# VectorE's state update moved ahead of its wait for GpSimd's power in the LSTM step

## The chip, the cores and the metric

One core of one Trainium2 chip runs the whole kernel, once. The metric is device microseconds for that launch; lower is better. Times given as a median are over 3 runs, and the profile is one further execution with its own time.

## What is computed

A vision-transformer-like tower over 128 images of 3 x 224 x 224: patches are projected to tokens, an LSTM runs over the 65 tokens of each image, and a mixture of 16 experts (top 2) follows. Cut to what matters:

```python
tokens = einsum('bpi,hi->bph', patches, W) + b           # 64 patches of 3*28*28 = 2352 values, 128 outputs
h0 = concat([cls, tokens], axis=1) * pos_embed            # 65 tokens
xg = einsum('btd,gd->btg', layernorm(h0), W_ih) + b_ih + b_hh
def step(carry, xt):                                      # 65 steps, one after the other
    h, c = carry
    i, f, g, o = split(xt + h @ W_hh.T, 4)
    c = sigmoid(f) * c + sigmoid(i) * tanh(g)
    h = sigmoid(o) * tanh(c)
    return (h, c), h
h1 = h0 + lstm                                            # residual
out = h1 + experts(layernorm(h1))                         # router, top 2 of 16, gelu in between
```

## The kernel before

The batch of 128 images fills the partitions. Each engine has a program of its own, written out by hand, and the engines meet only through semaphores; `through(engine, s, t)` waits until semaphore `s` has reached t + 1. Every engine runs its instructions strictly in the order of its program, so a wait holds up all that stands behind it.

The first 65 steps (n = 0 to 64) are the LSTM stage. A step n of the program works on several tokens at once, which is a software pipeline: token n in the LSTM recurrence, token n+1 and n+2 in the normalisation and the input gates, token n+3 in the patch projection, token n-1 and n-2 in the residual, the second normalisation and the router. From n = 61 the expert tiles join in, 80 tiles of 256 rows, and after the last step they run alone.

What each engine does in step n, in the order of its program:

- **TensorE**: the recurrent matmuls of token n (L1073 reads `h2_hi`, L1078 reads `h2_lo`), the transposition of the state h(n-1) (L1088), the transposition of the normalised row of token n-2 (L1098), the input-gate matmuls of token n+1 (L1106), the patch projection of token n+3 (L1063, 46 or more matmuls, the bulk of the step), the transposition of the normalised input `xn` of token n+2 (L1142), and the router (L1154). Just ahead of L1098 stands the wait for `xT_lo_done` of token n+1, so TensorE stops there when VectorE's `xT_lo` isn't ready.
- **ScalarE**: four tanh for the gates (L501), a copy `ynT` (L510), the first half of the split of the patches into two float16 parts (L484), the tanh of the cell `tc` (L520), the second half of the split (L484), the normalised row `pay` of token n-1 (L531, which needs `shift2`), the copy `xT_hi` (L538), and two copies of a piece of the expert weights (L544 and L545), which wait for that piece's DMA `ex_raw`. The gates of the next step stand behind them.
- **VectorE**: `xT_lo` (L639), the router's logits (now and then), the input row (L655), the residual row (L661), the statistics of both (L665 to L674), variance plus epsilon `veps` (L679), then `cab` and the cell `c2` (L683 and L686), then a wait for GpSimd's `rstd_done`, `shift2` (L690) and `xn` (L695), then the state as `h2_hi` (float16), `h2` and `h2_lo` (L700, L702, L706) behind a wait for `tc_done`, then `xlo` (L713), and last pieces of the routing (L762 and after, in most steps some three to five instructions). The next step begins with `xT_lo` again.
- **GpSimd**: `ex_lo` of a piece of the weights (L1001), the power -0.5 that gives `rstd` for two rows at once (L1008, waits for `veps`), and up to four indirect DMAs that send rows to the experts' lists (L1030).
- **SyncE** issues the loads: the patches of token n+6 (L365, L368, 1.2 MB), the positions (L391), the piece of weights n (L400).

The order of the state update against the normalised input is the order of the VectorE program in `step(n)`; nothing else decides it.

Of the kernel before, what the change touches and what calls it, by code (L numbers as in the profile page):

```python
# [83 lines left out]
def tower(nc, x, w, w_rest, cls, pos, w_ih, w_hh, b_ih, b_hh, rw, rb, we, b1, b2, const, out):  # L84
    F32, F16, I32 = mybir.dt.float32, mybir.dt.float16, mybir.dt.int32
    ALU, ACT, AX = mybir.AluOpType, mybir.ActivationFunctionType, mybir.AxisListType
    ctx = ExitStack()
    with ctx:
        def sb(name, shape, dt=F32):
            return ctx.enter_context(nc.sbuf_tensor(name, shape, dt))  # L90

        def sem(name):
            return ctx.enter_context(nc.semaphore(name))
# [34 lines left out]
        mv = sb("mv", [P, 2, 2])  # L128
        veps = sb("veps", [P, 2])
        rstd = sb("rstd", [P, 2])  # L130
        shift2 = sb("shift2", [P, 2])
        xn = sb("xn", [P, 2, HID])
# [113 lines left out]
        h0_done, xn_done = sem("h0_done"), sem("xn_done")  # L246
        st1, st2, moments = sem("st1"), sem("st2"), sem("moments")
        veps_done, rstd_done, shift_done = sem("veps_done"), sem("rstd_done"), sem("shift_done")
        xT_ps, xT_hi_done, xT_lo_done = sem("xT_ps"), sem("xT_hi_done"), sem("xT_lo_done")
# [86 lines left out]
        def through(eng, s, t):  # L336
            eng.wait_ge(s, (t + 1))

        def norms(n):

            there = [k for k, t in ((0, n + 2), (1, n - 1)) if 0 <= t <= T - 1]
            return slice(there[0], there[-1] + 1) if there else None

        def normed(n):

            return (n + 3)
# [250 lines left out]
        def _(dve):  # L597
# [37 lines left out]
            def step(n):  # L635
# [8 lines left out]
                t0, t1 = n + 2, n - 1  # L644
                pre, post = 0 <= t0 <= T - 1, 0 <= t1 <= T - 1
                if pre:

                    src0 = h0[:, t0 % 4, :]
# [26 lines left out]
                both = norms(n)  # L675
# [4 lines left out]
                if 0 <= n <= T - 1:  # L680
# [3 lines left out]
                                             ALU.mult).then_inc(cab_done, 1)  # L684
                    through(dve, cab_done, n)
                    dve.scalar_tensor_tensor(c2, cab[:, 0, :], 0.5, cab[:, 1, :], ALU.mult, ALU.add).then_inc(c_done, 1)  # L686
                if both:
                    dve.wait_ge(rstd_done, normed(n))
                if post:
                    dve.scalar_tensor_tensor(shift2[:, t1 % 2:t1 % 2 + 1], mv[:, 1, 0:1], -1.0, rstd[:, 1:2], ALU.mult,  # L690
                                             ALU.mult).then_inc(shift_done, 1)
                if pre:
                    if t0 >= 2:
                        through(dve, xT_ps, t0 - 2)
                    dve.tensor_scalar(xn[:, t0 % 2, :], src0, mv[:, 0, 0:1], rstd[:, 0:1], ALU.subtract,  # L695
                                      ALU.mult).then_inc(xn_done, 1)
                if 0 <= n <= T - 1:

                    through(dve, tc_done, n)
                    dve.scalar_tensor_tensor(h2_hi[:, n % 2, :], gate[:, 2, :], 1.0, tc[:, :], ALU.add,  # L700
                                             ALU.mult).then_inc(h_hi_done, 1)
                    dve.scalar_tensor_tensor(h2[:, n % 2, :], gate[:, 2, :], 1.0, tc[:, :], ALU.add,  # L702
                                             ALU.mult).then_inc(h_done, 1)
                    through(dve, h_hi_done, n)
                    through(dve, h_done, n)
                    dve.tensor_tensor(h2_lo[:, n % 2, :], h2[:, n % 2, :], h2_hi[:, n % 2, :],  # L706
                                      ALU.subtract).then_inc(h_lo_done, 1)
                t = n + 4
                if 1 <= t <= T - 1:

# [248 lines left out]
            def below_most():  # L959
# [3 lines left out]
                dve.tensor_tensor(top[:, 1, :], top[:, 1, :], top[:, 0, :], ALU.subtract).then_inc(under, 1)  # L963

            slots(step, step_b)

            dve.wait_ge(exp_done, 1)
# [304 lines left out]
```

## Time and profile before

| | |
|---|---|
| runs | 732.04 us median of 3 (730.67 to 735.34) |
| profiled execution | 732.84 us; its span from the first to the last instruction is 731.0 us |
| mean granted TensorE clock | 0.959 |
| TensorE, matmul | 630.0 us busy, 86% of the span |
| TensorE, weight load | 591.4 us, 81% |
| VectorE | 575.6 us, 79% |
| ScalarE | 488.3 us, 67% |
| GpSimd | 412.5 us, 56% |
| chain of work that ended last | TensorE 69%, issue 9%, DMA 7%, VectorE 5%, GpSimd 4% |

The LSTM stage takes the first 430 us or so of the span, the expert tiles most of the rest, and a last stage gathers the experts' results. The busy shares are averages over these stages. In the chain, "issue" is time for which the profile shows no releaser.

### The profile page before, as it was taken

How to read it: one execution, taken by the hardware profiler on the slowest of the kernel's cores; microseconds unless marked ns; L12 is line 12 of the kernel's file. 1: busy time of each engine (PE TensorE's matmuls, PEld its weight loads, DVE VectorE, ACT ScalarE, POOL GpSimd, SP SyncE). 2: the span in 40 equal slices, each digit the busy share in tenths (PEclk: the TensorE clock that was granted, in tenths of full speed). 3: DMA queues.
4: the chain of work that ended last, by engine and by line, in shares of the span. 5: the costliest groups of instructions: out<-in, count | busy, mean ns of one | idle time of the engine just before them, and what ended most of it. 6: DMA issues, size and time to landing. Idle time of an engine off the chain costs nothing.

```text
span 731.0 us, 25050 instructions
## 1 busy us (share of the span) xinstructions
PE 630.0 (86%) x7952; PEld 591.4 (81%) x7952; DVE 575.6 (79%) x1839; ACT 488.3 (67%) x1335; POOL 412.5 (56%) x446
## 2 busy tenths in 40 slices
PE   3999999999999999898988758899899999999500
PEld 3989989999989999898988737787799899899400
DVE  4577888787987887888888858887788888888587
ACT  4366666666666666666565556787788888888565
POOL 0122224766766767668367767777666666676600
PEclk9999999999999999999999969999999999999955
DMA  8767777877777778778674322455443333343097
GB/s 320 277 233 250 239 237 233 261 247 260 254 253 250 250 248 263 237 235 262 210 250 141 82 57 76 123 153 147 139 116 113 105 109 105 99 116 94 13 375 322
DMA packets 72188, 141.72 MB, mean 194 GB/s; under 512 B 13110, under 2 KB 55682, under 8 KB 63870
## 3 DMA queue, kind: packets, MB, share of 16 engines
q1 hardware_dynamic: 62416, 121.69, 52.2%
q0 software_dynamic: 9280, 17.21, 6.6%
q8 instruction: 70, 1.15, 0.6%
q10 hardware_dynamic: 366, 1.21, 0.5%
q14 instruction: 56, 0.46, 0.2%
HBM read 116.35 MB, written 25.66 MB: 194 GB/s over the span
## 4 chain that ended last, share of the span: by engine, by line
PE 69%; issue 9%; DMA 7%; DVE 5%; POOL 4%; SPq 2%; ACT 2%; POOLq 0%; ACTq 0%; DVEq 0%
PE bank L1063 28%; PE bank L1206 13%; PE bank L1223 12%; PE bank L1106 5%; PE bank L1073 3%; POOL sent L1030 3%; DMA patches<-back 2%; PE bank L1180 2%; DMA ex_raw<-in_we 2%; PE bank L1078 2%; PE bank L1098 2%; DMA patches<-in_x 1%; DMA patches<-sent 1%; PE bank L1154 1%; PE bank L1142 1%
## 5 line engine op out<-in xcount | busy, mean ns | idle before, releaser
L1041 POOL DMA_INDIRECT back<-patches x160 | 156.7, 979 | 70.7 <-issue 57.5
L1063 PE MATMUL bank<-ws,patches 128*128 128x128 f32 (+1 forms) x1408 | 176.7, 283 | 11.5 <-DMA patches<-in_x 11.5
L1030 POOL DMA_INDIRECT sent<-pay,slot_own x130 | 156.6, 1205 | 40.4 <-issue 39.8
L1063 PEld LDWEIGHTS bank<-ws,patches 128*128 128x128 f32 (+1 forms) x1408 | 167.4, 197 | 11.8 <-issue 9.2
L556 ACT ACTIVATE bank<-bank,b1s 128x256 f32<-128x256 f32 x320 | 130.9, 453 | 46.5 <-PE bank L1206 46.4
L918 DVE TENSOR_TENSOR patches<-bank,patches 128x512 f16<-128x512 f32 x160 | 109.7, 686 | 30.4 <-ACT patches L565 22.7
L1206 PE MATMUL bank<-patches,ex_hi 128*128 128x256 f16 x640 | 113.0, 278 | 5.0 <-POOL ex_lo L1001 2.9
L1223 PE MATMUL bank<-ex_hi,patches 128*128 x1280 | 111.7, 219 | 3.7 <-DVE patches L934 3.1
L1001 POOL TENSOR_TENSOR ex_lo<-ex_raw,ex_hi 128x256 f16<-128x256 f32 x64 | 44.2, 690 | 111.7 <-ACT ex_raw L545 111.5
L565 ACT ACTIVATE patches<-bank 128x512 f16<-128x512 f32 x160 | 97.6, 611 | 0.0
L1223 PEld LDWEIGHTS bank<-ex_hi,patches 128*128 128x128 f16 x1280 | 87.1, 98 | 8.0 <-issue 5.4
L1063 PE MATMUL bank<-whi,xhi 128*128 128x128 f16 x512 | 89.6, 220 | 0.0
L1063 PE MATMUL bank<-whi,xlo 128*128 128x128 f16 x512 | 89.3, 219 | 0.0
L1063 PE MATMUL bank<-wlo,xhi 128*128 128x128 f16 x512 | 89.3, 219 | 0.0
L1206 PE MATMUL bank<-patches,ex_lo 128*128 128x256 f16 x320 | 88.7, 277 | 0.0
L1223 PE MATMUL bank<-ex_lo,patches 128*128 x640 | 88.0, 219 | 0.0
L1008 POOL TENSOR_TENSOR rstd<-veps,cst 128x2 f32<-128x2 f32 (+1 forms) x68 | 52.6, 773 | 56.2 <-DVE veps L679 55.2
L484 ACT ACTIVATE xhi<-patches 128x512 f16<-128x512 f32 x128 | 80.5, 631 | 1.9 <-DMA patches<-in_x 1.7
L538 ACT ACTIVATE xT_hi<-bank 128x128 f16<-128x128 f32 x65 | 18.0, 276 | 90.9 <-PE bank L1142 87.2
L713 DVE TENSOR_TENSOR xlo<-patches,xhi 128x1024 f16<-128x1024 f32 x64 | 78.5, 1226 | 0.2
L1206 PEld LDWEIGHTS bank<-patches,ex_hi 128*128 x640 | 56.3, 99 | 24.2 <-issue 14.5
L501 ACT ACTIVATE gate<-bank,lbias 128x128 f32<-128x128 f32 x260 | 73.5, 364 | 2.3 <-PE bank L1078 2.3
(139 smaller groups left out, 1439.0 us busy)
## 6 DMA issues: line engine op xcount, KB each, us to landing
patches<-in_x SPq DMA_DIRECT2D x64, 1152.0 KB
patches<-sent SPq DMA_DIRECT2D x80, 130.0 KB
patches<-back SPq DMA_DIRECT2D x13, 640.0 KB, 6.4
ex_raw<-in_we SPq DMA_DIRECT2D x64, 128.0 KB
patches<-in_b SPq DMA_DIRECT2D x80, 64.0 KB
posr<-in_pos SPq DMA_DIRECT2D x65, 64.0 KB
out_tower<-h SPq DMA_DIRECT2D x13, 320.0 KB, 5.1
back<-patches POOLq DMA_INDIRECT x160
```

The lines of the kernel that those rows point to most:

```text
L484: return act.activation(xhi[r][:, a:b, :], xraw[q][:, a:b, :], ACT.Copy)
L501: last = act.activation(gate[:, GATE_AT[g], :], ps_gate[n % 2][:, g * B:(g + 1) * B], ACT.Tanh, bias=lbias[:, 2, g:g + 1], scale=(1.0 if g ...
L556: last = act.activation(up[:, cols], up[:, cols], ACT.Gelu, bias=b1s[:, bass.ds(e * FC + 2 * half + i, 1)], scale=1.0 / E_SCALE)
L565: act.activation(hhi[n % 4][:, half * 512:(half + 1) * 512], ps_up(n, half)[:, :], ACT.Copy).then_inc(hhi_done, 1)
L713: dve.tensor_tensor(xlo[r][:, :, :], xraw[q][:, 0:KS, :], xhi[r][:, :, :], ALU.subtract).then_inc(lo_done, 1)
L918: dve.tensor_tensor(hlo[n % 4][:, cols], ps_up(n, half)[:, :], hhi[n % 4][:, cols], ALU.subtract).then_inc(hlo_done, 1)
L1008: pool.tensor_tensor(rstd[:, both], veps[:, both], cst[:, C_POW:C_POW + 1].to_broadcast([P, both.stop - both.start]), ALU.pow).then_inc(rs ...
L1030: pool.indirect_dma_start(sent, bass.IndirectOffsetOnAxis(ap=slot_own[:, g % 4, k, col:col + 1], axis=0), pay[:, t % NP, :], None, bounds_ ...
L1041: pool.indirect_dma_start(back, bass.IndirectOffsetOnAxis(ap=dsti[j % NO][:, k:k + 1], axis=0), yo[j % NO][:, k, :], None, bounds_check=2 ...
L1063: last = pe.matmul(bank_of, l, w_, start=(c == KS and k == 0), stop=(c == KS - 1 and k == 2))
L1206: last = pe.matmul(ps_up(n, half)[:, i * ROWS:(i + 1) * ROWS], w1, r, start=(k == 0), stop=(k == 2))
L1223: last = pe.matmul(ps_down(j)[:, a * HID:(a + 1) * HID], h, w2, start=(c == 0 and k == 0 and a == 0), stop=(c == FC - 1 and k == 2), skip_ ...
```

## The change

In VectorE's `step(n)` the block that writes the state (`h2_hi`, `h2`, `h2_lo`) is moved from behind `shift2` and `xn` to a place ahead of the wait for `rstd_done`. The same instructions run with the same operands and the same waits; none is added or taken away, and the programs of the other engines stay as they were.

```diff
@@ -684,6 +684,17 @@
                     dve.scalar_tensor_tensor(c2, cab[:, 0, :], 0.5, cab[:, 1, :], ALU.mult, ALU.add).then_inc(c_done, 1)
+                if 0 <= n <= T - 1:
+
+                    through(dve, tc_done, n)
+                    dve.scalar_tensor_tensor(h2_hi[:, n % 2, :], gate[:, 2, :], 1.0, tc[:, :], ALU.add,
+                                             ALU.mult).then_inc(h_hi_done, 1)
+                    dve.scalar_tensor_tensor(h2[:, n % 2, :], gate[:, 2, :], 1.0, tc[:, :], ALU.add,
+                                             ALU.mult).then_inc(h_done, 1)
+                    through(dve, h_hi_done, n)
+                    through(dve, h_done, n)
+                    dve.tensor_tensor(h2_lo[:, n % 2, :], h2[:, n % 2, :], h2_hi[:, n % 2, :],
+                                      ALU.subtract).then_inc(h_lo_done, 1)
                 if both:
                     dve.wait_ge(rstd_done, normed(n))
                 if post:
@@ -694,17 +705,6 @@
                         through(dve, xT_ps, t0 - 2)
                     dve.tensor_scalar(xn[:, t0 % 2, :], src0, mv[:, 0, 0:1], rstd[:, 0:1], ALU.subtract,
                                       ALU.mult).then_inc(xn_done, 1)
-                if 0 <= n <= T - 1:
-
-                    through(dve, tc_done, n)
-                    dve.scalar_tensor_tensor(h2_hi[:, n % 2, :], gate[:, 2, :], 1.0, tc[:, :], ALU.add,
-                                             ALU.mult).then_inc(h_hi_done, 1)
-                    dve.scalar_tensor_tensor(h2[:, n % 2, :], gate[:, 2, :], 1.0, tc[:, :], ALU.add,
-                                             ALU.mult).then_inc(h_done, 1)
-                    through(dve, h_hi_done, n)
-                    through(dve, h_done, n)
-                    dve.tensor_tensor(h2_lo[:, n % 2, :], h2[:, n % 2, :], h2_hi[:, n % 2, :],
-                                      ALU.subtract).then_inc(h_lo_done, 1)
```

## Rows read from the trace of the kernel before

**Rows 1.** Busy time, 100 to 200 us (PE, PEld, DVE, ACT, POOL, clock, DMA share, GB/s)

```profile
100.00:200.00 100.00, 95.11 (x1238) 93.32 (x1237) 82.51 (x296) 64.70 (x200) 60.62 (x65) 1.00 0.75 249
```

**Rows 2.** TensorE's waits, whole span (us in total, times, longest)

```profile
PE bank L1098 <- issue: 24.4, 24, 2.3
PE bank L1073 <- DVE h_hi L700: 2.7, 1, 2.7
```

**Rows 3.** VectorE's and ScalarE's waits, from 30 to 400 us

```profile
DVE cab L683 <- ACT gate L501: 28.0, 24, 2.3
DVE shift L690 <- POOL rstd L1008: 11.6, 33, 1.9
...
ACT ex_hi L544 <- DMA ex_raw<-in_we: 35.5, 35, 2.6
```

**Rows 4.** Timeline, VectorE and TensorE, step 43 (start us, us, engine, line)

```profile
290.98 0.43 DVE L683 SCALAR_TENSOR_TENSOR cab<-gate 128x256 f32<-128x256 f32 x1 [1.60 <-ACT gate L501]
...
291.44 0.29 DVE L686 SCALAR_TENSOR_TENSOR gate<-cab 128x128 f32<-128x128 f32 x1
...
292.11 0.29 DVE L700 SCALAR_TENSOR_TENSOR h_hi<-gate,tc 128x128 f16<-128x128 f32 x1
...
292.81 0.28 PE L1142 MATMUL bank<-cst,xn 128*128 128x128 f32 x1
...
292.92 1.28 DVE L713 TENSOR_TENSOR xlo<-patches,xhi 128x1024 f16<-128x1024 f32 x1
...
295.48 0.28 DVE L639 TENSOR_TENSOR xT_lo<-bank,xT_hi 128x128 f16<-128x128 f32 x1
...
295.86 0.30 PE L1098 MATMUL bank<-cst,pay 128*128 128x128 f32 x1 [1.84 <-issue]
```

**Rows 5.** First and last of the 17 stalls behind an early step, TensorE's timeline

```profile
39.65 0.30 PE L1098 MATMUL bank<-cst,pay 128*128 128x128 f32 x1 [0.91 <-DVE xT_lo L639]
...
379.86 0.30 PE L1098 MATMUL bank<-cst,pay 128*128 128x128 f32 x1 [1.57 <-issue]
```

**Rows 6.** Timeline, GpSimd and VectorE, step 49 and (last row) step 50

```profile
328.62 0.85 POOL L1001 TENSOR_TENSOR ex_lo<-ex_raw,ex_hi 128x256 f16<-128x256 f32 x1
...
328.98 0.64 DVE L686 SCALAR_TENSOR_TENSOR gate<-cab 128x128 f32<-128x128 f32 x1
...
330.23 0.16 DVE L690 SCALAR_TENSOR_TENSOR shift<-mv,rstd 128x1 f32<-128x1 f32 x1 [0.62 <-POOL rstd L1008]
...
330.57 0.28 DVE L700 SCALAR_TENSOR_TENSOR h_hi<-gate,tc 128x128 f16<-128x128 f32 x1
...
331.37 1.22 DVE L713 TENSOR_TENSOR xlo<-patches,xhi 128x1024 f16<-128x1024 f32 x1
...
335.21 0.16 DVE L690 SCALAR_TENSOR_TENSOR shift<-mv,rstd 128x1 f32<-128x1 f32 x1 [0.29 <-POOL rstd L1008]
```

**Rows 7.** Timeline, step 51, and TensorE's stall at the head of step 52

```profile
340.31 0.29 DVE L686 SCALAR_TENSOR_TENSOR gate<-cab 128x128 f32<-128x128 f32 x1
...
341.77 0.72 POOL L1008 TENSOR_TENSOR rstd<-veps,cst 128x2 f32<-128x2 f32 x1
...
342.53 0.16 DVE L690 SCALAR_TENSOR_TENSOR shift<-mv,rstd 128x1 f32<-128x1 f32 x1 [1.92 <-POOL rstd L1008]
...
343.66 1.22 DVE L713 TENSOR_TENSOR xlo<-patches,xhi 128x1024 f16<-128x1024 f32 x1
...
346.88 0.45 PE L1098 MATMUL bank<-cst,pay 128*128 128x128 f32 x1 [2.30 <-issue]
```

**Rows 8.** Busy time in the stretch behind that stall (clock 0.63)

```profile
346.90:351.00 4.10, 4.10 (x30) 4.05 (x31) 3.64 (x15) 2.13 (x5) 2.43 (x3) 0.63 0.72 261
```

**Rows 9.** Timeline around steps 63 and 64: VectorE, GpSimd, TensorE

```profile
422.61 0.16 DVE L690 SCALAR_TENSOR_TENSOR shift<-mv,rstd 128x1 f32<-128x1 f32 x1 [2.24 <-POOL rstd L1008]
...
428.26 0.70 POOL L1001 TENSOR_TENSOR ex_lo<-ex_raw,ex_hi 128x256 f16<-128x256 f32 x1
...
429.96 0.60 PE L1206 MATMUL bank<-patches,ex_hi 128*128 128x256 f16 x2 [2.95 <-POOL ex_lo L1001]
```

## The prediction

> **What bounds the kernel now.** I read the busy shares and the chain first: TensorE leads, with 69% of the chain. I then read the stages. In the LSTM stage TensorE is 95% busy and VectorE 83%, at the full clock, 2.4 GHz [rows 1]. So a step lasts what TensorE's own work needs, plus its stalls. TensorE's waits say where these are: 24 times, 24.4 us in total, ahead of L1098 [rows 2]. The profile names no releaser for them, but the program does: ahead of L1098 stands the wait for `xT_lo`, the first instruction of VectorE's step. Laid side by side, VectorE writes `xT_lo` from 295.48 to 295.76 us and TensorE goes on at 295.86 after 1.84 us of idle time [rows 4]. TensorE isn't waiting for the state; it waits for VectorE to reach the end of its step.
>
> VectorE's waits tell why it is late [rows 3]. In 24 steps between 30 and 400 us `cab` waited for the gates, because ScalarE had waited for a piece of the expert weights (35 waits, 35.5 us). I call these steps **early**, since in them `rstd` is there before `c2`. In 33 steps VectorE waited for `rstd`: 11.6 us in all. The timelines split these into 30 waits of at most 0.30 us, as in step 50, and three **late** ones: 0.62 us in step 49, 1.92 in step 51 and 0.62 in step 57, when GpSimd's row sends and `ex_lo` ran over [rows 6, 7]. Step 61 repeats step 49.
>
> **The change, part by part.** Nothing is added; only VectorE's order changes. I measure how long VectorE needs from the end of `c2` to the start of `xlo`.
>
> - Before, early step: 292.92 - 291.73 = 1.19 us [rows 4]. `tc` takes ScalarE's tanh, so `h2_hi` can't start before 0.38 us after `c2` (292.11 - 291.73), and `shift2` and `xn` fill just this gap. The three state instructions then take 0.81 us.
> - `shift2` and `xn` cost VectorE 330.57 - 330.23 = 0.34 us [rows 6].
> - After: 0.38 us of idle time, 0.81 for the state, 0.34 for `shift2` and `xn`: 1.53 us, unless `rstd` comes later than 1.19 us after `c2`.
>
> So an early step gets 0.34 us longer: the filler is taken out of the gap. An ordinary step (0.29 us of wait, then 331.37 - 330.23 = 1.14 us from `shift2` to `xlo`, together 1.43) gets 0.10 longer [rows 6]. Step 49 took 331.37 - 329.62 = 1.75 us and gets 0.22 shorter, and 57 and 61 likewise. Step 51 took 343.66 - 340.60 = 3.06 us; with `shift2` at 342.53 and 0.34 behind it, it takes 2.27, so 0.79 shorter [rows 7].
>
> What reaches TensorE depends on the slack ahead of `xT_lo`. I went through the timelines of all steps. 17 of the 24 early steps are followed by a stall, so that VectorE's end sets it (the first and the last in [rows 5]): 17 x 0.34 = 5.8 us. The other seven have 0 to 0.5 us of slack; I take 1.2 us for them together. Most ordinary steps have 0.1 to 1.6 us of slack before ScalarE's `xT_hi` is there; some seven have none: 0.5 us. The late steps give back 3 x 0.22 + 0.79 = 1.5 us.
>
> The stall of 2.30 us at the head of step 52 is followed by a stretch with a granted clock of 0.63 [rows 7, 8], that is, partly at 1.2 GHz. TensorE is busy for all of its 4.10 us, so the clock costs 4.10 x (1 - 0.63) = 1.5 us. With 0.79 us less, its stall is 1.5 us, and behind the stalls of 1.84 us [rows 4] and 1.57 [rows 5] the clock stayed full. I count this 1.5 us as won.
>
> Queued behind the moved instructions: `xn` now ends some 1.6 us after `c2`, and TensorE reads it at L1142. In ordinary steps that is over a microsecond early enough. In ten early steps it is late, as in step 43: 291.73 + 1.6 = 293.35 against 292.81 [rows 4]. TensorE then stalls 0.1 to 1.25 us in front of L1142. That costs nothing more, since TensorE stalls anyway a little later for `xT_lo`, and that stall shrinks by the same amount; in all ten it is long enough or short by under 0.1. ScalarE's `pay` waits for `shift2`, now about 0.9 us later, and `xT_hi` and the copies of the weights stand behind it; in ordinary steps ScalarE has 1.5 us idle there. GpSimd's program doesn't wait for what moved. SyncE's patch load waits for `xlo` of two steps before, and its queue is unaffected.
>
> At the end of the stage VectorE waited 2.24 us for `rstd` in step 63, and TensorE 2.7 us for `h2_hi` [rows 2, 9]. That wait goes, but the expert tiles start when GpSimd has written the last `ex_lo`, 428.96 us, behind its row sends; TensorE then resumes at 429.96 [rows 9]. What is late next is GpSimd, so 2.7 us of stall are worth nothing. In step 64 VectorE does 0.8 us of state work ahead of time, of which TensorE sees 0.15 to 0.2.
>
> Sum: 5.8 + 1.2 + 0.5 - 1.5 - 1.5 - 0.2 = **+4.3 us**. The profiled execution took 732.84 us and would take 737.1. It lies 0.8 above the median of 732.04, so for a median I forecast **736.3 us**.
>
> One rule speaks against the gain of the late steps. The trace first: L686 took 0.64 us in step 49, where GpSimd's `ex_lo` was running, and 0.29 in step 51 [rows 6, 7]. The Trainium skill, SBUF — State Buffer, "Who interferes with whom", says that a VectorE instruction with two SBUF inputs contends with a GpSimd instruction that reads SBUF, and that the later one waits. The trace agrees. By that rule the state instructions, moved beside the power, would lengthen by up to 0.35 us in steps 49, 57 and 61, and the sum would be +5.3 instead of +4.3.
>
> **The rivals.**
>
> - *The DMA sets the pace.* If the weight pieces land at their own rate, each 0.34 us added to a step shortens a later wait of ScalarE. The 35 waits [rows 3] could absorb all 7.5 us, and the gains of 3.2 stay: 732.04 - 3.2 = 728.8 us, on the faster side. It decides once more than 4.3 of the 7.5 is absorbed. For it: DMA is 75% busy [rows 1], and the waits come every two or three steps. Against it: a load is issued relative to TensorE's step, and most waits are longer than 0.34 us and recur after stalls that cleared the queues.
> - *More stalls cross into the lower clock.* Steps 12, 43 and 56 would stall 2.0, 2.2 and 1.8 us, between 1.84 (full clock) and 2.30 (0.63). Each crossing costs 1.5 us; with two, and no gain at step 52: 736.3 + 4.5 = 740.8 us.
> - *The wait for `xn` adds up.* If it doesn't come out of the later stall, ten waits of 0.6 us on average cost 6 us or more: 742 us or above. Against it: `xT_lo` hangs on VectorE's end, not on L1142, in these steps.
> - *GpSimd is late far more often than this execution shows.* Each step like 51 gives 0.8 us and perhaps 1.5 of clock; it takes five more of them to be over 1% faster. The trace has one.
>
> **How the numbers follow.** My forecast, 733 to 739 us: 0.50. Absorbed by the DMA, 728.8 to 733: 0.25. Clock or added waits, above 739: 0.20. Late GpSimd, below 728.8: 0.05. The range takes in most of the first three, 729.5 to 741.5. About 1%, 7.3 us, is what a measurement of this kernel can tell from no change. Below 724.7: 0.05. Above 739.4: 0.16. Within: 0.79.
>
> **What would show it.** In the profile after, each early step should have 1.53 us from `c2` to `xlo`, with 0.38 idle ahead of `h2_hi`. VectorE's wait for `rstd` at L690 should all but vanish, being left in steps 51, 63 and 64. TensorE should have new waits ahead of L1142, and those at L1098 should not shrink by more than that. The clock behind step 51 should stay full. I am wrong if the weights' waits fall by some 4 us or more, if the clock dips elsewhere, or if TensorE's total stall in the LSTM stage doesn't grow by about 6 us.

## The result, and the profile after

| | before | after |
|---|---|---|
| median | 733.87 us (728.96 to 738.33, 15 runs) | 738.01 us (733.85 to 743.10, 15 runs) |
| ratio of the two | | 1.005, 95% interval 1.0028 to 1.0073 |
| profiled execution | 732.84 us, span 731.0 | 735.97 us, span 734.2 |
| mean granted TensorE clock | 0.959 | 0.956 |

The change makes the kernel 4.1 us slower (738.01 - 733.87); 4.3 us were forecast. It is inside the 1% that the prediction called no change, but the interval leaves 1.000 out. The ratios here and below leave out the few executions that were slow as a whole, so they need not equal the quotient of two medians.

In the kernel after, `h2_hi`, `h2` and `h2_lo` are L690, L692 and L696, `shift2` is L701 and `xn` L706. First one early step, to hold against [rows 4]. The timeline of the kernel after, VectorE and TensorE, step 43 (start us, us, engine, line, operation, in brackets the idle time before it and what ended it):

```profile
294.22 0.42 DVE L683 SCALAR_TENSOR_TENSOR cab<-gate 128x256 f32<-128x256 f32 x1 [1.24 <-ACT gate L501]
294.68 0.29 DVE L686 SCALAR_TENSOR_TENSOR gate<-cab 128x128 f32<-128x128 f32 x1
295.34 0.29 DVE L690 SCALAR_TENSOR_TENSOR h_hi<-gate,tc 128x128 f16<-128x128 f32 x1 [0.38 <-ACT tc L520]
296.15 0.15 DVE L701 SCALAR_TENSOR_TENSOR shift<-mv,rstd 128x1 f32<-128x1 f32 x1
296.22 0.34 DVE L706 TENSOR_SCALAR xn<-h,mv,rstd 128x128 f32<-128x128 f32 x1
...
296.48 1.22 DVE L713 TENSOR_TENSOR xlo<-patches,xhi 128x1024 f16<-128x1024 f32 x1
...
296.61 0.33 PE L1142 MATMUL bank<-cst,xn 128*128 128x128 f32 x1
...
298.81 0.28 DVE L639 TENSOR_TENSOR xT_lo<-bank,xT_hi 128x128 f16<-128x128 f32 x1
...
299.19 0.30 PE L1098 MATMUL bank<-cst,pay 128*128 128x128 f32 x1 [1.32 <-issue]
```

VectorE stands 0.38 us idle ahead of `h2_hi` for the tanh behind `c2`, and `h2_hi` begins at the same distance as before. From the end of `c2` (294.97) to `xlo` (296.48) it is 1.51 us, where it was 1.19. The gap that `shift2` and `xn` filled is now empty, and they are paid for behind it. TensorE still stops ahead of L1098 until VectorE's `xT_lo` is there.

VectorE's, TensorE's and ScalarE's waits in the kernel after, from 30 to 400 us (us in total, times, longest), to hold against [rows 3] and, for L1098, [rows 2]:

```profile
ACT ex_hi L544 <- DMA ex_raw<-in_we: 30.1, 31, 2.3
ACT pay L531 <- DVE shift L701: 29.0, 57, 0.5
...
DVE cab L683 <- ACT gate L501: 26.8, 26, 2.4
...
DVE h_hi L690 <- ACT tc L520: 22.1, 59, 0.4
PE bank L1098 <- issue: 16.0, 15, 2.8
...
PE bank L1142 <- DVE xn L706: 4.7, 8, 1.3
```

VectorE's wait for `rstd`, 11.6 us in 33 steps before, is gone from this stretch altogether. What took its place is larger: 22.1 us in 59 steps, the tanh's gap, which was full of work before. ScalarE's `pay` now waits for `shift2`. TensorE has a new wait ahead of L1142, as forecast, and the one ahead of L1098 is smaller by about as much. The steps that VectorE's lateness starts in are still there (26 waits of `cab` for the gates).

Where the 4 us lie can be read off the start of the first recurrent matmul (L1073) of a step. The last column is ScalarE's waits for the weights up to step 47. "e1" to "e12" are the experiments below:

| kernel | step 1 to 48 | 48 to 54 | 54 to 64 | start of 64 | waits for weights |
|---|---|---|---|---|---|
| before | 287.7 | 39.2 | 64.1 | 423.0 | 29.7 us, 28 |
| after | 292.3 | 36.6 | 66.0 | 426.0 | 24.4, 22 |
| e1, before, weights early | 271.0 | 37.7 | 64.3 | 405.4 | none |
| e2, after, weights early | 272.2 | 35.4 | 63.0 | 401.8 | none |
| e3, before, power twice | 294.6 | 41.8 | 71.8 | 441.1 | 25.0, 25 |
| e4, after, power twice | 292.5 | 40.0 | 64.1 | 428.2 | 29.6, 29 |
| e5, third order, weights early | 271.0 | 36.8 | 63.8 | 403.6 | none |
| e6, third order | 298.2 | 37.7 | 66.0 | 433.0 | 33.2, 26 |
| e7, before, power first, weights early | 282.2 | 37.5 | 66.0 | 416.8 | none |
| e8, third order, power first, weights early | 290.5 | 41.8 | 69.8 | 432.9 | none |
| e9, after again | 302.9 | 42.0 | 66.3 | 442.4 | 28.0, 24 |
| e10, before again | 292.5 | 38.1 | 66.9 | 428.5 | 31.7, 24 |
| e11, before, 0.34 us more on VectorE | 300.1 | 42.2 | 67.8 | 442.2 | 31.6, 28 |
| e12, third order again | 295.9 | 37.9 | 66.0 | 432.3 | 30.8, 29 |

In the first pair the change costs 4.6 us up to step 48, where the early and ordinary steps are, gains 2.6 between 48 and 54, where GpSimd was late before, and loses 1.9 behind that: together 3.9 us. The start of step 64 moves by 3.0 us only and the span by 3.2, because step 1 started 1.0 us sooner in this execution (31.1 against 32.1 us). Step 0 already did (25.3 against 26.3), ahead of the first use of the moved block, so that 1.0 us is not of the change.

The loss from 54 to 64 has a place of its own. TensorE's timeline in the kernel after, at the head of step 57, and its busy time ahead of that stall and behind it (PE, PEld, DVE, ACT, POOL, granted clock, DMA share, GB/s):

```profile
382.70 0.30 PE L1098 MATMUL bank<-cst,pay 128*128 128x128 f32 x1 [2.83 <-issue]
```

```profile
372.00:381.90 9.90, 7.87 (x111) 7.62 (x108) 8.37 (x29) 6.07 (x19) 7.17 (x9) 1.00 0.76 218
381.90:386.00 4.10, 3.30 (x22) 3.33 (x23) 3.52 (x17) 1.79 (x5) 2.25 (x3) 0.62 0.72 278
```

This is the dip of [rows 8] (0.63), moved from step 52 to step 57: TensorE stood idle for 2.83 us and its clock then averaged 0.62, so part of that stretch ran at 1.2 GHz. Over step 57 it averaged 0.83, which over the step's 10.3 us is a loss of 1.7 us. Behind step 51 the clock stayed at its full 2.4 GHz, as forecast. Part of that long stall is a piece of the routing that met GpSimd. VectorE's and GpSimd's timelines of the kernel after:

```profile
380.90 1.37 DVE L870 TENSOR_TENSOR tabs<-tabs 128x16 f32<-128x16 f32 x2
...
381.55 0.69 POOL L1001 TENSOR_TENSOR ex_lo<-ex_raw,ex_hi 128x256 f16<-128x256 f32 x1
```

The same two instructions took 0.38 us in step 55. Beside `ex_lo` they took 1.37 us, and `xT_lo` stands behind them.

### The profile page after: what moved, and what is told of

It reads as the page before. It is cut to its first block, busy times and chain, and to the rows that moved or that the text cites. A ratio compares the mean times of both kernels' runs of the same rounds, so it can differ in the third digit from the quotient of the medians.

```text
span 734.2 us, 25050 instructions
## 1 busy us (share of the span) xinstructions
PE 632.9 (86%) x7952; PEld 592.1 (81%) x7952; DVE 576.2 (78%) x1839; ACT 494.0 (67%) x1335; POOL 406.6 (55%) x446
## 4 chain that ended last, share of the span: by engine, by line
PE 28%; DMA 6%; issue 5%; DVE 4%; SPq 3%; POOL 2%; ACT 2%; POOLq 0%; ACTq 0%; DVEq 0%
PE bank L1206 13%; PE bank L1223 12%; DMA patches<-back 3%; PE bank L1180 2%; POOL sent L1030 2%; DMA patches<-sent 1%; DMA ex_raw<-in_we 1%; ACT patches L592 1%; SPq L428 0%; DVE h L986 0%; SPq L437 0%; SPq L409 0%; SPq L410 0%; SPq L438 0%; SPq L429 0%
## 5 line engine op out<-in xcount | busy, mean ns | idle before, releaser
L1063 PE MATMUL bank<-ws,patches 128*128 128x128 f32 (+1 forms) x1408 | 176.2, 282 | 11.6 <-DMA patches<-in_x 11.6
L1030 POOL DMA_INDIRECT sent<-pay,slot_own x130 | 150.0, 1154 | 40.5 <-issue 38.6
L918 DVE TENSOR_TENSOR patches<-bank,patches 128x512 f16<-128x512 f32 x160 | 109.6, 685 | 30.8 <-ACT patches L565 23.8
```

The source lines that it names most:

```text
L918: dve.tensor_tensor(hlo[n % 4][:, cols], ps_up(n, half)[:, :], hhi[n % 4][:, cols], ALU.subtract).then_inc(hlo_done, 1)
L1030: pool.indirect_dma_start(sent, bass.IndirectOffsetOnAxis(ap=slot_own[:, g % 4, k, col:col + 1], axis=0), pay[:, t % NP, :], None, bounds_ ...
L1063: last = pe.matmul(bank_of, l, w_, start=(c == KS and k == 0), stop=(c == KS - 1 and k == 2))
```

## Experiments

Each ratio is to the kernel before, run on the same chip in the same series. On the chips of e5 to e8 and e9 to e12 the kernel before itself took 837.37 and 840.10 us (medians), against 733.87 and 737.15 on the first two; nearly all of the difference lies behind the LSTM stage (last section). So times of different series are not compared, only ratios and the stages of the table above.

### Are the early steps the cause? e1 and e2: weights loaded one step sooner

Early steps exist because ScalarE waits for a piece of the expert weights. Both kernels get the same edit in SyncE's program; e1 has VectorE's order of before, e2 that of the change:

```diff
-                if 0 <= n <= PIECES - 1:
-                    if n >= 4:
-                        through(sp, ex_lo_done, n - 4)
-                    sp.dma_start(ex_raw[:, n % 4, :], we[:, bass.ds(n * PIECE, PIECE)]
-                                 ).then_inc(ex_in[n % 4], 16)
+                piece = n + 1
+                if 0 <= piece <= PIECES - 1:
+                    if piece >= 4:
+                        through(sp, ex_lo_done, piece - 4)
+                    sp.dma_start(ex_raw[:, piece % 4, :], we[:, bass.ds(piece * PIECE, PIECE)]
+                                 ).then_inc(ex_in[piece % 4], 16)
```

> The kernel before, but SyncE issues the load of each piece of the expert weights one step earlier. My theory: ScalarE's waits for these pieces (35.5 us in 35 waits) make the early steps, in which the gates come late while rstd is ready. They should all but vanish (under 5 us), the 24 waits of cab for the gates too, and the time should fall by 8 to 18 us. Rival, the DMA sets the pace: the waits move elsewhere and the time falls by less than 3 us.

> The same earlier load, with the changed order. My theory: the change costs 0.34 us in early steps and 0.08 to 0.10 in ordinary ones with mostly slack behind them. Without early steps it should cost no more than 2 us against the kernel before with the earlier load, and could gain 1. Rival: the cost is there in every step, whether or not the gates are late; then the 4 us stay.

Measured: e1 715.70 us (714.73 to 718.48, 4 runs), ratio 0.9722 (0.9644 to 0.9801). e2 713.25 us (710.96 to 713.70, 4 runs), ratio 0.9680 (0.9606 to 0.9754). Both beat both kernels. e1's time fell by 21.5 us (737.15 - 715.70), more than the 8 to 18 expected. The ranges of the runs of e1 and e2 do not overlap, though they are of four runs each, and the changed order is now the faster one by 2.4 us, where 1 at most had been expected.

Waits from 30 to 400 us, first e1, then e2 (all lines lie 1 higher than in before and after):

```profile
DVE shift L691 <- POOL rstd L1009: 21.3, 62, 1.9
...
PE bank L1099 <- issue: 8.5, 7, 2.4
```

```profile
DVE h_hi L691 <- ACT tc L521: 23.3, 62, 0.4
...
PE bank L1099 <- issue: 5.9, 6, 2.0
```

Neither kernel has a wait of ScalarE for weights or of `cab` for gates: every step is ordinary or late. Up to step 48 the changed order still costs 1.2 us (272.2 against 271.0). From 48 to 54 it gains 2.3 and from 54 to 64 1.3. So without early steps the sign turns, as the prediction's sum has it: its 7.0 us from early steps fall out, and the 0.5 of the ordinary and the gains of the late ones stay.

### Does the change do what it says where GpSimd is late? e3 and e4: the power computed twice

GpSimd computes the power once more into a spare tile ahead of the real one. This is extra work; nothing is left out. e3 has the order of before, e4 that of the change:

```diff
+                    pool.tensor_tensor(spare[:, both], veps[:, both],
+                                       cst[:, C_POW:C_POW + 1].to_broadcast([P, both.stop - both.start]),
+                                       ALU.pow)
```

> The kernel before, with GpSimd computing the power once more into a spare tile ahead of the real one, so that rstd comes 0.7 to 0.8 us later in every step. My theory: ordinary steps wait some 1.0 us at L690 instead of 0.3 and the time grows by 8 to 20 us. Rival: VectorE's wait doesn't reach TensorE and the time grows by under 3 us.

> The same doubled power, with the changed order. My theory: rstd now comes about 1.0 us after c2, still ahead of the 1.19 us at which the state is written, so nothing more is waited for; the time is 737 to 741 us, 6 to 15 us below the doubled power in the old order. That is where the change pays. Rival: the change costs its 4 us whatever rstd does, and the time is 4 us above that of the old order with the doubled power.

Measured: e3 754.40 us (749.70 to 757.92, 4 runs), ratio 1.0238 (1.0139 to 1.0336). e4 740.03 us (735.76 to 744.15, 10 runs), ratio 1.0042 (1.0006 to 1.0078). The changed order is 14.4 us faster here.

The waits of e3 from 30 to 400 us, and one of them in VectorE's timeline; then the same wait in e4:

```profile
DVE shift L691 <- POOL rstd L1012: 45.2, 57, 2.6
```

```profile
242.91 0.16 DVE L691 SCALAR_TENSOR_TENSOR shift<-mv,rstd 128x1 f32<-128x1 f32 x1 [0.96 <-POOL rstd L1012]
```

```profile
DVE shift L702 <- POOL rstd L1012: 1.8, 2, 0.9
```

With `rstd` 0.96 us after `c2` instead of 0.29, the order of before pays 45.2 us of waiting, and the changed order 1.8: its state work covers up to 1.19 us. The rival that the change costs its 4 us whatever `rstd` does falls. But the waits on VectorE are not what reaches the end: between step 1 and 48, where most of the 45.2 us lie, the two profiled executions are only 2.1 us apart (294.6 and 292.5), while 1.8 us lie between 48 and 54 and 7.7 between 54 and 64, where GpSimd is late. Up to step 48 the rest falls into time in which TensorE didn't need VectorE, or comes off ScalarE's waits for the weights, which are 4.6 us shorter in e3 than in e4; the runs don't part the two. What the change lacks in the real kernel is a wait to cover: 0.29 us, less than the 0.38 us that the tanh takes anyway.

### Is it the order, or the late `xn`? e6, e5 and e12: a third order

The state's first two instructions go ahead of the wait for `rstd`, and `h2_lo` stays behind `xn`. So `shift2` and `xn` stand between `h2` and `h2_lo`, which waits for `h2` in any case:

```diff
+                if 0 <= n <= T - 1:
+
+                    through(dve, tc_done, n)
+                    dve.scalar_tensor_tensor(h2_hi[:, n % 2, :], gate[:, 2, :], 1.0, tc[:, :], ALU.add,
+                                             ALU.mult).then_inc(h_hi_done, 1)
+                    dve.scalar_tensor_tensor(h2[:, n % 2, :], gate[:, 2, :], 1.0, tc[:, :], ALU.add,
+                                             ALU.mult).then_inc(h_done, 1)
                 if both:
                     dve.wait_ge(rstd_done, normed(n))
...
                 if 0 <= n <= T - 1:
-
-                    through(dve, tc_done, n)
-                    dve.scalar_tensor_tensor(h2_hi[:, n % 2, :], gate[:, 2, :], 1.0, tc[:, :], ALU.add,
-                                             ALU.mult).then_inc(h_hi_done, 1)
-                    dve.scalar_tensor_tensor(h2[:, n % 2, :], gate[:, 2, :], 1.0, tc[:, :], ALU.add,
-                                             ALU.mult).then_inc(h_done, 1)
                     through(dve, h_hi_done, n)
```

e6 is this alone, e5 has the weights a step early too.

> Weights one step early, and a third order: h2_hi and h2 ahead of the wait for rstd as in the changed kernel, then shift2 and xn, and h2_lo behind them, so that shift2 and xn fill the 0.18 us in which h2_lo waits for h2. My theory: from c2 to xlo it takes 1.35 us, against 1.51 in the changed order and 1.43 in ordinary steps of the old one; with VectorE's end setting about a third of the steps this gives 1 to 4 us over the changed order with the early weights (713.2). Rival: TensorE has slack there, and the time is the same within 1 us.

> The third order alone, with the weights loaded as before. My theory: early steps cost 1.35 us against 1.19 before and 1.51 in the changed kernel, ordinary and late ones are shorter than before: the time lies 0 to 2 us above the kernel before, at least 1 us below the changed one. Rival, the loss of the change isn't the VectorE time of the early steps but the late xn or the late state: then it is as slow as the changed kernel, or slower since the state's low part comes later still.

Measured: e5 810.64 us (809.26 to 813.65, 4 runs), ratio 0.9664 (0.9630 to 0.9699). e6 840.63 us (834.59 to 843.78, 10 runs), ratio 1.0030 (1.0000 to 1.0059). From `c2` to `xlo` both take 1.31 us, 0.20 less than the changed order: the time in which `h2_lo` waited for `h2` is now used. e6 lies 0.30% above the kernel before, some 2.5 us, a little over the 0 to 2 expected, and its interval overlaps that of the change (1.0028 to 1.0073): by itself it doesn't tell the third order from the changed one. e5 has the lowest ratio of all, but its interval covers e2's 0.9680, so which of the two is better is not settled.

e12 repeats e6 beside the kernel after (e9), the kernel before (e10) and e11, all on one chip.

> The third order with the weights loaded as before, on the chip of the changed kernel's repeat. My theory: 1 to 3 us below the changed kernel, since from c2 to xlo it takes 1.31 us against 1.51. Rival, the late state and xn themselves cost: not below it.

Measured: 838.82 us (835.50 to 845.90, 10 runs), ratio 0.9986 (0.9959 to 1.0013), against 1.0096 for e9: the third order is as fast as the kernel before within 0.4%, and about 1.1% faster than the changed order on the same chip, with intervals that do not meet. 1 to 3 us had been expected; 1.1% is 9 us. So the third order doesn't win: it undoes the loss. `xn` ends 154.04 - 152.84 = 1.20 us after `c2` in it, where the changed order has 296.56 - 294.97 = 1.59 (step 43 above); before, TensorE could already use it 292.81 - 291.73 = 1.08 us after `c2` [rows 4]. VectorE's timeline of e12, an early step:

```profile
152.55 0.29 DVE L687 SCALAR_TENSOR_TENSOR gate<-cab 128x128 f32<-128x128 f32 x1
153.22 0.29 DVE L691 SCALAR_TENSOR_TENSOR h_hi<-gate,tc 128x128 f16<-128x128 f32 x1 [0.38 <-ACT tc L521]
...
153.63 0.15 DVE L698 SCALAR_TENSOR_TENSOR shift<-mv,rstd 128x1 f32<-128x1 f32 x1
153.70 0.34 DVE L703 TENSOR_SCALAR xn<-h,mv,rstd 128x128 f32<-128x128 f32 x1
```

### How much of added VectorE time arrives? e9, e10 and e11

e9 is the kernel after again, e10 the kernel before again (one run). e11 is the kernel before with one more VectorE instruction, shaped like `xn` and written to a spare tile, behind `h2_lo` in every step:

```diff
+                    if n >= 1:
+                        dve.tensor_scalar(spare[:, :], h1[:, n - 1, :], mv[:, 0, 0:1], rstd[:, 0:1], ALU.subtract,
+                                          ALU.mult)
```

> The changed kernel once more, so that it stands on one chip with the three others here. Theory: a ratio of 1.003 to 1.007 to the kernel before.

> The kernel before once more, for its profile on this chip, to see how far the count of early steps and stalls (24 and 17 in the first profile, ScalarE's waits for the weights 35.5 us) repeats. Theory: 20 to 30 early steps, waits of 30 to 42 us, first recurrent matmul of step 48 within 4 us of 320 us.

> The kernel before with one more VectorE instruction, the shape of xn into a spare tile, behind h2_lo in each step: 0.26 to 0.34 us more VectorE work in all steps, in the place where the change puts its extra time. If all of it that finds no slack reached the end, it would cost 7 + 2.5 + 1 = about 10 us (24 early, 30 ordinary, 4 late steps). If later weight waits give back a third, as the profile of the changed kernel suggests, 6 to 8 us. Rival, the DMA sets the pace: under 3 us.

Measured: e9 851.64 us (840.06 to 858.24, 10 runs), ratio 1.0096 (1.0045 to 1.0148), above the 1.003 to 1.007 expected, with an interval that overlaps the first pair's. e10 832.69 us, one run; the 23 runs of the kernel before in this series have a median of 840.10 and go from 833.40 to 845.64, so e10 is faster than all of them, and differences to its profile come out large. e11 848.05 us (844.82 to 852.87, 8 runs), ratio 1.0099 (1.0065 to 1.0132). VectorE's timeline of e11, an ordinary step:

```profile
158.72 0.16 DVE L691 SCALAR_TENSOR_TENSOR shift<-mv,rstd 128x1 f32<-128x1 f32 x1 [0.29 <-POOL rstd L1012]
...
159.06 0.28 DVE L701 SCALAR_TENSOR_TENSOR h_hi<-gate,tc 128x128 f16<-128x128 f32 x1
...
159.85 0.34 DVE L710 TENSOR_SCALAR spare<-h,mv,rstd 128x128 f32<-128x128 f32 x1
```

The instruction adds 0.26 us from `c2` to `xlo` (1.44 against 1.18 in early steps), and by the medians the kernel gets 848.05 - 840.10 = 8.0 us slower, as expected. The two profiled executions lie 15.8 us apart (848.45 - 832.69), 7.6 of them between step 1 and 48 (300.1 against 292.5). Over 47 steps 0.26 us make 12.2 us, so six tenths arrive in this pair of executions. That isn't the DMA setting the pace: under that theory under 3 us were expected. The waits of e10 and e11 for the weights are alike (31.7 and 31.6 us).

e9 against e10 costs 10.3 us between step 1 and 48, where the first pair (before and after) cost 4.6. But 3.4 of the 10.3 are TensorE's clock. It fell in steps 18 and 36 of e9, and between step 1 and 48 not at all in e10, in before or in after. Those two steps of e9 (columns as above):

```profile
136.10:143.80 7.70, 7.57 (x79) 7.40 (x78) 6.03 (x21) 3.96 (x12) 4.59 (x5) 0.78 0.57 201
254.70:263.20 8.50, 7.52 (x79) 7.35 (x78) 6.70 (x23) 4.04 (x12) 3.56 (x5) 0.80 0.60 192
```

7.70 x 0.22 and 8.50 x 0.20 are 1.7 us each. That is the prediction's rival of more stalls that cross into the lower clock. It came true in this execution, and the third order's have such dips too: e6 two between step 1 and 48, e12 one. None of the six profiles with the order of before has one there. That the new orders make them likelier is suggested by this, not shown: after, e2, e4, e5 and e8 have none there either. Without its two dips e9 lost 6.9 us against e10. The prediction had 7.5 for early and ordinary steps. The waits for weights fell by 5.3 us in the first pair and by 3.7 in this one. That they give a part back holds in both; how large a part differs from execution to execution, more than one profile can tell.

### Is the wait better shortened at its source? e7 and e8: GpSimd's power ahead of `ex_lo`

In GpSimd's program the power goes ahead of `ex_lo`, so that it is never late behind it. e7 has VectorE's order of before, e8 the third order, both with the weights a step early:

```diff
+                both = norms(n)
+                if both:
+                    pool.wait_ge(veps_done, normed(n))
+                    if n - 1 >= 1:
+                        through(pool, yn_done, n - 2)
+                    pool.tensor_tensor(rstd[:, both], veps[:, both],
+                                       cst[:, C_POW:C_POW + 1].to_broadcast([P, both.stop - both.start]),
+                                       ALU.pow).then_inc(rstd_done, 1)
...
-                both = norms(n)
-                if both:
-                    pool.wait_ge(veps_done, normed(n))
```

> Weights one step early, the old order on VectorE, and on GpSimd the power ahead of ex_lo, so that in the steps where GpSimd has run over rstd comes 0.65 us less late. My theory: what the changed order gains with the early weights (2.4 us) comes from these late steps, so this takes 1 to 3 us off 715.7 without touching VectorE: 712.7 to 714.7, with waits of about 1.25 us where there were two of 1.92. Rival: the late steps don't matter, no change within 0.5 us.

> All three together: weights early, third order, power first. My theory: the two cures of the late steps overlap, so that it gains no more than 1 us over the third order with early weights. Rival: they add, and it is 2 us or more below it.

Measured: e7 824.44 us (822.77 to 829.05, 4 runs), ratio 0.9853 (0.9805 to 0.9900). e8 843.01 us (840.46 to 847.86, 9 runs), ratio 1.0080 (1.0052 to 1.0108). Both expectations were missed: e7 should have been 1 to 3 us below e1, and takes 11.2 us more from step 1 to 48 (e1 ran on another chip, but e5 on e7's chip took the same 271.0 us there); e8 should have been like e5, and takes 19.5 more. The table of lines from 60 to 360 us, `shift2` in e1 and then in e7 (busy us, mean ns, then the idle time before them), and both engines' timelines in e7:

```profile
L691 DVE SCALAR_TENSOR_TENSOR shift<-mv,rstd 128x1 f32<-128x1 f32 x51 | 8.1, 160 | 17.6 <-POOL rstd L1009 17.6
```

```profile
L691 DVE SCALAR_TENSOR_TENSOR shift<-mv,rstd 128x1 f32<-128x1 f32 x49 | 30.8, 628 | 15.9 <-POOL rstd L1000 15.9
```

```profile
249.10 0.66 POOL L1010 TENSOR_TENSOR ex_lo<-ex_raw,ex_hi 128x256 f16<-128x256 f32 x1
...
249.15 0.63 DVE L691 SCALAR_TENSOR_TENSOR shift<-mv,rstd 128x1 f32<-128x1 f32 x1 [0.29 <-POOL rstd L1000]
```

The swap puts `ex_lo` beside `shift2` in every step. `shift2`, one element a partition, takes 628 ns instead of 160 and ends with `ex_lo`. From `c2` to `xlo` it is 1.92 us instead of 1.42. This is the contention that the prediction read in L686 [rows 6], now in each of the steps. In e8 it is `h2_hi` that meets `ex_lo`, in the table of lines of the same stretch:

```profile
L691 DVE SCALAR_TENSOR_TENSOR h_hi<-gate,tc 128x128 f16<-128x128 f32 x47 | 23.1, 491 | 17.6 <-ACT tc L521 17.6
```

Its mean is 491 ns instead of 292. It took some 640 ns beside `ex_lo`, in about half the steps, and these need 1.65 to 1.72 us from `c2` to `xlo`; the others need 1.36. That is some 0.35 us in half of 47 steps, about 8 us; VectorE's `xT_lo` also waits more for ScalarE. What makes up the rest of its 19.5 us is open.

## Why the prediction was right

Direction, mechanism and range held. The closeness of 4.1 to 4.3 us is luck, since two terms failed in opposite directions: the loss in the early and ordinary steps came out 2.9 us too small in the first pair, and the gain behind them 2.3 too small. All three signs that the prediction had named for being wrong appeared as well: the waits for the weights fell by 5.3 us, the clock dipped elsewhere, and TensorE's stall didn't grow by 6 us (up to step 48 its listed waits grew by 0.9, from 14.2 to 15.1, and the steps themselves by 4.6).

- **What bounds the stage.** TensorE waits ahead of L1098 for the end of VectorE's step: held. e11 lengthens VectorE alone and the kernel gets 8.0 us slower.
- **Durations in an early step.** Forecast 1.53 us from `c2` to `xlo` with 0.38 idle; measured 1.51 with 0.38.
- **Early and ordinary steps, 5.8 + 1.2 + 0.5 = 7.5 us.** In the first pair the stage with nearly all of them grew by 4.6 us, so the term was too large there: the waits for weights shrank by 5.3 us and so, it seems, gave a part back; no run parts this from the scatter of single executions. The prediction had put this down as a rival and as nothing in its sum. In the second pair the stage grew by 6.9 us without the clock's 3.4, and the waits shrank by 3.7. Split by VectorE's step ahead (a stall at L1142 counted with the early step that causes it; the split moves with where the line between early and ordinary is drawn), about 1 to 1.7 us of the 4.6 lie behind early steps and 2 to 2.7 behind ordinary ones; of the 6.9 it is 3.5 to 4.6 and 1 to 2.3, and the rest is step 1. Neither looks like the forecast's 7.0 and 0.5: the early term was too large and the ordinary one too small in both. Cause and sign are shown by e1 and e2 (without early steps the loss is gone) and by e12 (with most of the gap used otherwise it is gone too); the size of the term is known to some 3 us either way.
- **Ordinary steps, 0.10 us each.** e1 against e2 has 1.42 and 1.51 us from `c2` to `xlo`, and 1.2 us over 47 steps, all ordinary. The 0.10 us on VectorE held; what arrives is more than the 0.5 us of the sum.
- **Late steps, 1.5 us.** Before, steps 49, 51 and 57 took 1.75, 3.06 and 1.76 us; after, 1.51 in all three. In step 51 2.27 were forecast: `cab` itself waited 1.11 us for the gates in that step, and `rstd` was there by then. In e2, where that wait is missing, steps 49 and 51 take 2.34 and 2.36 instead of 3.07 and 3.06, which is 0.73 and 0.70 where 0.79 was forecast.
- **The clock, 1.5 us won behind step 51.** It was won there and lost again at step 57, where "if the clock dips elsewhere" had been named as a way to be wrong. The two stages together, from 48 to 64, changed by -2.6 + 1.9 = -0.7 us where -3.0 had been forecast. The term that failed is this one: a stall that has got shorter in one place doesn't buy the clock for the whole kernel. Its premise failed too. The prediction let the length of the stall decide (a full clock behind 1.84 us, 0.63 behind 2.30), and the experiments' traces go against it. At the head of step 52 e1 stood idle longer than before, and its clock stayed full; e4 stood 1.89 us there and 1.81 in step 57, and both times the clock fell. The stall and the stretch behind it, in e1 and then in e4:

```profile
330.51 0.30 PE L1099 MATMUL bank<-cst,pay 128*128 128x128 f32 x1 [2.40 <-issue]
330.50:334.60 4.10, 4.09 (x49) 4.09 (x50) 3.64 (x15) 2.12 (x5) 2.40 (x3) 1.00 0.67 245
```

```profile
351.84 0.31 PE L1102 MATMUL bank<-cst,pay 128*128 128x128 f32 x1 [1.89 <-issue]
351.80:355.90 4.10, 4.06 (x28) 4.09 (x29) 3.55 (x15) 2.23 (x5) 2.56 (x3) 0.58 0.73 272
```

  What decides whether a stall is followed by a dip is open here.
- **The tail, -0.2 us.** TensorE's waits of the kernel after from 400 to 450 us:

```profile
PE bank L1142 <- DVE xn L706: 2.3, 1, 2.3
...
PE bank L1073 <- DVE h_hi L690: 1.4, 1, 1.4
```

  The 2.7 us at L1073 [rows 2] became 1.4, and the wait for `xn` in step 62 grew from 1.44 to 2.3 us: what is gained at one place goes at another. The kernel behind the start of step 64 takes 308.1 us after and 308.0 before: no gain of 0.2 can be seen, and the term is too small to be judged.
- **L1142.** Forecast: ten waits, taken out of those ahead of L1098. Measured: eight, 4.7 us, and the listed waits at both places add up to 21.0 us after (16.0 + 4.7 + 0.3) and 21.3 before (20.4 + 0.9), from 30 to 400 us. Held. That the sum of the listed waits doesn't grow is no sign that nothing was lost: short ones are left out of the list. Measured by the steps' lengths, the time above 5.68 us a step (the shortest usual step), from step 1 to 48, went from 20.8 to 25.4 us; the steps shorter than 5.75 us fell from 18 to 10, and those of 5.75 to 6.1 rose from 11 to 18.
- **The rival of contention (+5.3).** The trace shows that what stretches the state's instructions is `ex_lo`, not the power. e2, VectorE and GpSimd in a late step, and e4 beside a power:

```profile
323.99 0.72 POOL L1002 TENSOR_TENSOR ex_lo<-ex_raw,ex_hi 128x256 f16<-128x256 f32 x1
...
324.11 0.75 DVE L693 SCALAR_TENSOR_TENSOR h<-gate,tc 128x128 f32<-128x128 f32 x1
```

```profile
239.89 0.69 POOL L1012 TENSOR_TENSOR rstd<-veps,cst 128x2 f32<-128x2 f32 x1
...
240.03 0.29 DVE L691 SCALAR_TENSOR_TENSOR h_hi<-gate,tc 128x128 f16<-128x128 f32 x1 [0.38 <-ACT tc L521]
```

  `h2` took 0.75 us instead of 0.28 beside `ex_lo`; `h2_hi` took its usual 0.29 beside the power, which reads two elements a partition, while beside `ex_lo` the same instruction took some 0.64 (e8). In e2's late step the 0.47 us cost nothing, since `rstd` was later still.

  The Trainium skill, SBUF — State Buffer, "Who interferes with whom", lets any GpSimd instruction that reads SBUF contend with a VectorE instruction of two SBUF inputs. The trace agrees for `ex_lo` and does not for the small power; the measurement decides.

## What to carry to other kernels

Before a wait is covered by moving work ahead of it, look at what stands in that work's own shadow: here the consumers of `rstd` filled the 0.38 us in which the tanh ran, and a wait of 0.29 us was cheaper than the hole they left. A reordering pays from the point at which the awaited value is later than that gap (e3 against e4, 14.4 us, of which the stage with the many ordinary waits gave 2.1 and the one where GpSimd is late 7.7), and the same two kernels can stand either way round depending on something far from the edit (e1 against e2: a load issued one step sooner). The larger gain lay in that load, 2.8 to 3.4%, and it was to be seen in the waits of before [rows 3] as ScalarE's 35.5 us.

## What the runs showed of the hardware

**A VectorE instruction of one element a partition was held for nearly all of a GpSimd instruction.** `shift2` took 160 ns alone and 628 ns beside `ex_lo` (e7, 49 times in 300 us), and a pair of 128x16 instructions 1.37 us instead of 0.38. e7 lost 11.2 us against e1 in 47 steps with no work added.

**The same kernel took 100 us more on two other chips, nearly all of it behind the LSTM stage.** The busy time of the kernel before from 500 to 600 us, first in its first profile, then in e10 (columns as above):

```profile
500.00:600.00 100.00, 96.47 (x1231) 85.78 (x1230) 81.86 (x196) 82.11 (x195) 67.35 (x69) 1.00 0.43 120
```

```profile
500.00:600.00 100.00, 80.06 (x945) 65.38 (x946) 61.53 (x156) 61.85 (x145) 48.63 (x50) 1.00 0.36 103
```

TensorE runs 945 matmuls there instead of 1231, at a full clock. Behind the start of step 64 e10 takes 402.3 us where before took 308.0, and up to it 428.5 where before took 423.0. With the weights a step early the stage up to step 48 is the same on both kinds of chip (271.0 us in e1 and in e5). It held for every kernel of those two series: 402 to 412 us behind that point, against 307 to 310 in the first two. Its cause wasn't tried and is open.
